# A recurrence on eight columns: one PSUM bank per gate, inputs grouped in one step, expert work woven into the routing

## The reference, cut to what matters

```
for t in range(256):                       # h: 8 batches x 128
    r = sigmoid(x[t] @ W_ir + b_ir + h @ W_hr)
    z = sigmoid(x[t] @ W_iz + b_iz + h @ W_hz)
    n = tanh(x[t] @ W_in + b_in + r * (h @ W_hn + b_hn))
    h = (1 - z) * n + z * h
# every token (2048 of them): softmax over h @ router_w.T, top-1 expert;
# an expert takes at most 320 tokens, those of highest probability,
# and the rest go to expert 0
# y = relu(h @ W1[e] + b1[e]) @ W2[e] + b2[e],  W1 128x512, W2 512x128
```

## Time and profile before

| | us |
|---|---|
| median of 3 runs (lowest to highest) | 1527.37 (1525.01 to 1528.93) |
| the profiled execution, its own time | 1528.47 |
| its span, first to last instruction | 1526.7 |
| PE busy in the span | 1403.5 (92%) |
| DVE, ACT, POOL busy | 715.6, 673.6, 146.7 |
| mean granted TensorE clock | 0.944 of full speed |
| DMA, mean over the span | 18 GB/s |

### The profile page before, as it was taken

One profiled execution on the slowest core, in us unless ns is written; L12 is line 12 of the kernel. 1 busy time (PEld: TensorE's weight loads), 2 busy tenths in 40 slices (PEclk: granted clock), 3 DMA queues, 4 the chain that ended last, 5 costly groups with the idle time before them and its releaser, 6 DMA issues. The chain is left out here.

```text
span 1526.7 us, 29728 instructions
## 1 busy us (share of the span) xinstructions
PE 1403.5 (92%) x10828; PEld 1104.6 (72%) x10829; DVE 715.6 (47%) x2422; ACT 673.6 (44%) x2429; POOL 146.7 (10%) x236
## 2 busy tenths in 40 slices
PE   7999988999989999999999997699999999838994
PEld 4333333777769999999999983488888888735663
DVE  3476765545543454444544526532333333672223
ACT  3322213556534666666666641243434443623442
POOL 4000003000000000000000000110000000325652
PEclk9899989999999999999999986697999999968997
DMA  5000000000021000000000000100000000001113
GB/s 164 1 1 0 1 0 1 1 1 1 1 70 43 2 1 2 2 2 2 2 2 2 2 1 1 35 22 22 23 23 22 23 9 2 12 18 38 42 42 98
DMA packets 27834, 27.93 MB, mean 18 GB/s; under 512 B 2381, under 2 KB 22346, under 8 KB 27562
## 3 DMA queue, kind: packets, MB, share of 16 engines
q1 hardware_dynamic: 21082, 16.71, 3.7%
q0 software_dynamic: 2496, 5.12, 1.2%
q10 hardware_dynamic: 4112, 4.19, 0.9%
HBM read 21.36 MB, written 4.65 MB: 17 GB/s over the span
## 5 line engine op out<-in xcount | busy, mean ns | idle before, releaser
L1698 PE MATMUL spare<-identb 128*128 128x128 bf16 x2996 | 215.1, 223 | 0.0
L1698 PEld LDWEIGHTS spare<-identb 128*128 128x128 bf16 x2996 | 198.6, 106 | 4.7
L1186 ACT ACTIVATE ghid<-gh_ps,cols 128x128 f32<-128x128 f32 x512 | 160.3, 364 | 63.7 <-PE gh_ps L1094 63.7
L1094 PE MATMUL gh_ps<-hist,w 128*128 128x128 f32 x1024 | 160.5, 278 | 2.9 <-ACT ghid L1186 2.9
L1104 PE MATMUL gy_ps<-w2e,ghid 128*128 128x128 f32 x1024 | 156.2, 275 | 0.5 <-ACT ghid L1186 0.3
L1094 PEld LDWEIGHTS gh_ps<-hist,w 128*128 128x128 f32 x1024 | 136.5, 189 | 5.3 <-ACT ghid L1186 5.2
L1104 PEld LDWEIGHTS gy_ps<-w2e,ghid 128*128 128x128 f32 x1024 | 135.5, 191 | 0.9 <-ACT ghid L1186 0.5
L1147 PE MATMUL pre_z<-hist,gru_w 128*128 128x128 f32 x512 | 121.5, 318 | 0.0
L1758 DVE TENSOR_TENSOR_SCAN targ<-gates,pairs 128x16 f32<-128x16 f32 x256 | 49.1, 192 | 149.0 <-ACT gates L1708 149.0
L1655 PEld LDWEIGHTS s_pre<-s,wT 128*128 128x128 f32 x512 | 80.1, 197 | 42.1 <-ACT s L1711 40.1
L1655 PE MATMUL s_pre<-s,wT 128*128 128x8 f32 x512 | 100.7, 269 | 4.4 <-ACT s L1711 2.7
(11 more groups left out here) (422 smaller groups left out, 2458.8 us busy)
## 6 DMA issues: line engine op xcount, KB each, us to landing
w<-in_L_ffn_W SPq DMA_DIRECT2D x1, 2048.0 KB, 9.6
raw<-in_L_ffn_wg SPq DMA_DIRECT2D x8, 256.0 KB, 3.1
raw<-in_L_ffn_wu SPq DMA_DIRECT2D x8, 256.0 KB, 3.1
raw<-in_L_ffn_wd SPq DMA_DIRECT2D x8, 256.0 KB, 2.6
wqkv<-in_L_attn_Wqkv SPq DMA_DIRECT2D x1, 1536.0 KB, 6.3
mrow<-mt SPq DMA_DIRECT2D x8, 128.0 KB, 1.8
y_top<-yrow SPq DMA_DIRECT2D x4, 256.0 KB, 5.4
y_next<-yrow ACTq DMA_DIRECT2D x4, 256.0 KB, 6.2
```

The lines of the kernel that those rows point to most:

```text
L1094: mm = nc.tensor.matmul(h_ps[:, f % 2, :], w1[:, e, P * f:P * f + P], tokens(grp), start=True, stop=True)
L1186: nc.scalar.activation(hid[v % 2][:, f, :], h_ps[:, f % 2, :], ACT.Relu, bias=n.cols[:, at:at + 1]).then_inc(h_done, 1)
L1698: nc.tensor.matmul(spare[:, 0:P], n.identb[:, :], n.identb[:, :], start=True, stop=True)
```

## The change

`gru_scan` and `route_top1` become one function, `recurrence`.

- A gate has one bank instead of two, and `pre_z` is a product of 8 columns as the other two are. `hist` is no longer set to zero but for its first step.
- The seven input products of the next group are issued together behind step 15 of a group, each gate's behind a wait for the engine that last read that gate's bank. There is no expert step in that step of the recurrence. So 225 of the 260 expert steps lie within the recurrence (there were 240).
- `gh_ps` and `gy_ps` have two banks each within the recurrence and one afterwards. The transposes, choices and logits share another bank in four slots.
- The logits: POOL copies each finished group of 16 steps into `hB` in another layout (16 copies of 128 by 128), and the router's products take their weights from there; the 8 blocks of the first half are woven into the recurrence, one at a time, and 8 are left behind the last step.
- The other 35 expert steps are woven into the routing: 2, 4 and 2 into its first block, one for each of the 24 pieces into the second, and 3 behind them. `rows` has two buffers instead of three.
- `picks` and `parts` have 128 columns instead of 24, with zeros in the rest, and so have the transposes and the products made of them.

```diff
+    def expert_step(s):
+        return (s // G - 1) * (G - 1) + s % G if s >= G and s % G != FREE else None
...
+                @block.gpsimd
+                def _(pool):
...
+                    for g in range(GROUPS):
+                        pool.wait_ge(state, G * (g + 1) + 1)
+                        pool.tensor_copy(hB[:, :, G * g:G * g + G], tokens(g).rearrange("p (t b) -> p b t", b=B)).then_inc(turned_b, 1)
...
+                    def inputs(g, s):
...
+                        if s >= 0:
+                            pe.wait_ge(r_done, s + 1)
+                        nc.tensor.matmul(pre_r[:, 0:P], n.gru_w[:, 0, :], x, start=True, stop=False, skip_group_check=True)
+                        nc.tensor.matmul(pre_r[:, 0:P], n.bias_parts[:, 1, :], n.ones_b[:, :], start=False, stop=False, skip_group_check=True)
...
                         pe.wait_ge(state, s + 1)
-                        for out, i, rhs, ready in ((gate_slot(pre_r, s), 3, now, r_pre), (first(n_slot(s)), 5, now, n_pre),
-                                                   (z_out, 4, h, z_pre)):
-                            nc.tensor.matmul(out, n.gru_w[:, i, :], rhs, start=False, stop=True,
+                        for out, i, ready in ((gate_slot(pre_r, s), 3, r_pre), (first(n_slot(s)), 5, n_pre), (gate_slot(pre_z, s), 4, z_pre)):
+                            nc.tensor.matmul(out, n.gru_w[:, i, :], now, start=False, stop=True,
                                              skip_group_check=True).then_inc(ready, 1)
...
+                        if s % G == FREE:
+                            if s // G + 1 < GROUPS:
+                                inputs(s // G + 1, s)
+                        elif s < G:
+                            for _ in range(FILL):
+                                nc.tensor.matmul(y_bank[0][:, 0:P], n.identb[:, :], n.identb[:, :], start=True, stop=True)
+                        else:
+                            w = expert_step(s)
...
+                            expert_products(pe, w)
+                            grp, k = divmod(w, G)
+                            if GROUPS // SEG + 2 <= grp < GROUPS // SEG + 2 + B // 2 and k in (8, 12):
...
+                                block_logits(SEG * (2 * (grp - GROUPS // SEG - 2) + (k == 12)))
...
                 @block.tensor
                 def _(pe):
-                    for src, dst, ready in ((picks, tq, 6), (parts, tp, 14)):
+                    w = w0
+                    for src, dst, ready, ahead in ((picks, tq, 6, EARLY), (parts, tp, 14, MIDDLE)):
+                        for _ in range(ahead):
+                            expert_products(pe, w)
+                            w += 1
                         pe.wait_ge(step, ready)
...
+                    step_no = w1st
                     for r in range(NP):
                         i, c0, w, _ = pieces[r]
+                        if step_no < STEPS:
+                            expert_products(pe, step_no)
+                            step_no += 1
                         pe.wait_ge(counted, r + 1)
+                        if r + 2 < NP:
+                            fill(r + 2)
...
-                        if r + 3 < NP:
-                            fill(r + 3)
```

More of the change, by code:

```diff
@@ L979, in _, with recurrence @@
                     add(b)
-def gru_scan(nc, n, a, hist, w1, w2, diffT, logits):
+def recurrence(nc, n, a, hist, w1, w2, diffT):
     G = P // B
@@ L1003, in sem, with bank @@
             return local.enter_context(nc.semaphore(name))
[L1005 to L1018, removed]
+        def bank(name, stack=local):
+            return stack.enter_context(nc.psum_tensor(name, [P, 512], F32))
+        h_bank, y_bank, turn = [bank("gh_ps0")], [bank("gy_ps0")], bank("g_turn")
+        slot = [turn[:, P * i:P * i + P] for i in range(4)]
         hid = [sb(f"ghid{i}", [P, NF, P]) for i in range(2)]
@@ L1047, in tokens @@
             return second(hist[:, 16 * (G * g + 1):16 * (G * (g + 1) + 1)])
[L1049 to L1140, removed]
@@ new lines, in expert_relu @@
+        def expert_relu(act, w):
+            if w >= HALVES:
+                return
+            v, half = divmod(w, 2)
+            e = v % E
+            act.wait_ge(h_in, w + 1)
+            if v >= 2:
+                act.wait_ge(y_in, v - 1)
+            for f in range(2):
+                at = b10 + NF * e + 2 * half + f
+                nc.scalar.activation(hid[v % 2][:, 2 * half + f, :], h_bank[w % len(h_bank)][:, P * f:P * f + P], ACT.Relu,
+                                     bias=n.cols[:, at:at + 1]).then_inc(h_done, 1)
@@ L1148, in _ @@
                                              skip_group_check=True).then_inc(ready, 1)
[L1149 to L1156, removed]
@@ L1170, in _ @@
+                    pe.wait_ge(state, T + 1)
+                    for b in range(B):
+                        mm = block_logits(SEG * b + 1)
+                    mm.then_inc(all_logits, 1)
+                @block.scalar
+                def _(act):
+                    act.preload_act_table(ACT.Sigmoid)
+                    act.wait_ge(const, 4)
+                    for s in range(T):
                         act.wait_ge(r_pre, s + 1)
@@ new lines, in _ @@
+                        w = expert_step(s)
+                        if w is not None:
+                            expert_relu(act, w)
+                @block.vector
+                def _(dve):
+                    V = nc.vector
+                    for i in range(2):
+                        V.memset(reset[i][:, :], 0.0)
+                        V.memset(fresh[i][:, :], 0.0)
+                        last = V.memset(mix[i][:, :], 0.0)
+                    V.memset(choice[:, :], 0.0)
+                    last.then_inc(const, 1)
+                    V.tensor_scalar(iota_m8[:, :], n.iota8[:, :], -float(E), None, ALU.add).then_inc(const, 1)
+                    V.tensor_scalar(zero_hot[:, :], n.iota8[:, :], 0.0, None, ALU.is_equal).then_inc(const, 1)
+                    V.memset(at_step(0), 0.0).then_inc(const, 1)
+                    dve.wait_ge(const, 4)
+                    V.tensor_copy(second(at_step(0)), n.condT).then_inc(state, 1)
+                    dve.wait_ge(state, 1)
+                    for s in range(T):
@@ L1274, in _ @@
-                    v = (s - G) // 2 - 1
-                    if k % 2 == 0 and 0 <= v < JOBS:
-                        add(v)
-                    if k == 0 and grp < GROUPS:
-                        choose(grp, 0)
-                    if k == 1 and grp < GROUPS:
-                        for i in range(1, 4):
-                            choose(grp, i)
-                    if s == T + 1:
-                        dve.wait_ge(all_logits, 1)
-                        V.tensor_copy(logits[:, :, :].rearrange("p i e -> p (i e)"), pre_r[0][:, 0:NBLK * E])
@@ L1402, in route_top1 @@
         NP = len(pieces)
+        w1st = w0 + EARLY + MIDDLE + LATE
         with ExitStack() as middle:
-            rows = [middle.enter_context(nc.psum_tensor(f"rows{i}", [P, PIECE], F32)) for i in range(3)]
+            rows = [middle.enter_context(nc.psum_tensor(f"rows{i}", [P, PIECE], F32)) for i in range(2)]
             sums = middle.enter_context(nc.psum_tensor("r_sums", [P, 512], F32))
```

369 lines of the change are left out of this document (220 added, 149 removed).

## The result

| | before | after |
|---|---|---|
| median of four runs on one chip, us | 1528.15 | 1864.16 |
| lowest to highest | 1525.01 to 1529.22 | 1861.83 to 1869.25 |
| span of the profiled execution | 1526.7 | 1867.4 |
| mean granted TensorE clock | 0.944 | 0.755 |

The ratio is 1.221, 95% interval 1.219 to 1.224. The forecast was 1507.4, in 1492 to 1527.

What follows compares the result with a forecast made beforehand. Plain steps were taken as bound by the state's chain, 0.06 us above TensorE's work. Terms -17.8 - 30.8 + 10.1 + 16.8 + 1.7 = -20.0 us on the 1527.4 median gave 1507.4, range 1492 to 1527.

Steps and rivals of the forecast that it cites:

- `pre_z` on 8 columns: Recurrence: dropping 120 columns shortens the product's end by about 0.10 us, gaining 0.065 us for each plain step.
- The clock falls inside the recurrence: Rival, recurrence: shorter `pre_z` lowers the clock; steps over 2 us, time far over 1600 us; chance 2%.
- the slower rival of the routing: Rival, routing behind the recurrence: woven work runs at 1.2 GHz, +33 us, so 1540; chance 0.11.
- recurrence: All groups of steps together: -17.8 us, from shorter plain steps and input products gathered into one step.
- behind the last step: Stage after the recurrence: 34.1 us replaced by 3.3 for the last copy and remaining logits, -30.8 us.
- first routing block: Routing's first block: eight added expert steps take it from 8.9 to 19 us, +10.1, between +6 and +13.
- loop of the second: Routing's second block, 24 pieces: TensorE becomes the limit at 1.6 us a piece; 27.3 to 44.1 us, +16.8.
- Plain step: Recurrence step without input products: 1.64 us set by the state's chain becomes 1.575, set by TensorE's 14 passes.
- Input step: Step 15 of a group, all inputs and no expert work: 1.59 to 1.77 us, 1.77 taken.
- The rival that the step stays at 1.64: Recurrence: the 128 columns weren't in the chain, so plain steps gain nothing; +14.6 us, 1522; chance 0.14.
- POOL's copies: Recurrence, 16 a group: about 0.35 us each, counted as nothing; up to 5.6 us worse if all contend with VectorE.
- "better weave" rival: Routing's second-block loop: coupling costs nothing and VectorE's 31.8 + 1 sets it; 11 us less, 1496; chance 0.12.

Runs made afterwards that it cites:

- experiments 2: Kernel before with only its update gate product `pre_z` narrowed to 8 columns: 1894.71 us, ratio 1.246.
- 7: Changed kernel with two 128-column bf16 fillers in each of the first 128 expert steps: 1884.36 us.
- experiment 1: Changed kernel with 72 small filler products at the head of TensorE's list of the recurrence: 1493.21 us, ratio 0.982.
- experiment 5: Changed kernel with 72 fillers at the recurrence's head and the update gate on 128 columns again: 1504.96 us, ratio 0.989.
- experiment 12: Changed kernel with 72 head fillers, routing's turned operands back on 24 rows: four executions, 1492.03, 1495.97, 1509.32 and 1514.92 us.
- experiment 11: Changed kernel with 72 head fillers plus fillers in TensorE's later idle stretches up to the next layer: 1491.83 us.
- experiment 6: Changed kernel with one burst of 80 fillers at the end of step 127: 1682.02 us.
- experiment 3: Changed kernel with its update gate on 128 columns again and the history zeroed beforehand: 1535.30 us, ratio 1.008.
- 9: Changed kernel with the first hidden product issued twice (float32) in the first 128 expert steps: 1575.43 us.
- 10: Changed kernel with twelve 128-column bf16 fillers in each of the first 32 expert steps: 1539.70 us, one execution; a second, 5889 us, left out.
- 4: Kernel before without the 16 fillers in each of its first 16 steps: 1535.49 us, ratio 1.009.

## Why the prediction was wrong

**The step that failed** is the first of the change, "*`pre_z` on 8 columns*", where I priced the 120 columns as the end of a product and nothing else, and its rival "*The clock falls inside the recurrence*", to which I gave 2% because "the expert products, which make up most of a step, are untouched". They are eight of 14 passes, and TensorE is always busy, and still such a step does not raise the clock (the changed kernel, experiments 2 and 7). In place of a plain step of 1.575 us the runs show one of 2.99, at 0.50 for 802 us, and a recurrence that is 352 us longer where the sum had -17.8. The price in the rival was right in kind: it had steps over 2 us, and a step at half clock is 14 passes at 0.2135, 2.99. Its mechanism was put wrongly: the clock doesn't fall in the recurrence, it is low on entry and is not raised. I argued from the stretch 762 to 890.7, where the clock had been full for 300 us, and never asked from what it had come up. The trace of before had the warning at 452.5: it enters low, and something in its first steps has to raise it. One row warned too. Behind the last step TensorE was busy for 10.2 us at 0.50 before the clock came back. I put that down to expert steps, to argue *against* the slower rival of the routing; but the first half of it, to 897.7, is the router's products, which are 8 columns wide.

The Trainium skill (TensorE: Matmul & The Clock Gate, "Why this matters for your kernels") says to keep TensorE continuously busy for full clock, and to avoid idle gaps. The second half agrees: behind the gap of 4.9 us ahead of the recurrence the clock is at 0.50 (from 452.5 in the kernel before). The first half doesn't hold here: TensorE is shown busy for all of 282.00 us (480 to 762) at 0.50.

**The other terms** can be read from experiment 1, which is the change at full clock, against the earlier trace rows:

| us | forecast | experiment 1 |
|---|---|---|
| recurrence | -17.8 | 415.2 - 435.1 = -19.9 |
| behind the last step | -30.8 | 3.4 - 34.1 = -30.7 |
| first routing block | +10.1 | 16.6 - 8.9 = +7.7 |
| loop of the second | +16.8 | 36.6 - 27.3 = +9.3 |
| end, to the next layer's first product | +1.7 | 11.9 - 9.0 = +2.9 |
| sum | -20.0 | -30.7 |

The two profiled executions are 33.9 us apart (1528.47 and 1494.56). The other 3.2 us lie outside the change: the first state comes 0.7 us later in experiment 1, and the layers behind the routing take some 4 us less; why was not followed.

- *Plain step* 1.575: right (1.57), and bound by TensorE. *Input step* 1.77: right (1.78). The rival that the step stays at 1.64 is refuted by experiment 5 against 1.
- *POOL's copies* are 0.40 each (0.35 taken). None of them overlaps an instruction of VectorE in experiment 1 or in the changed kernel, and the recurrence came out better than the sum: there is no loss of 5.6 us, but no run shows the two together either.
- *Behind the last step*: right; the 16 weight loads of the logits took 2.12 us, not 1.8.
- *First block*: within its bounds, at full clock but for its first 5.5 us.
- *Loop*: mis-sized. I had 1.6 a piece by TensorE, and 5.7 on top for coupling, start, once-a-group products and half clock. It measured 36.6 / 24 = 1.53 a piece, all included, 7.5 us less: TensorE's own work is 35.38, not 38.4, and all the rest is 1.2. That is the way of the "better weave" rival, but not its mechanism. It had VectorE as the limit, and VectorE is busy 31.34 of the 36.6 (31.8 forecast), while TensorE is the limit still.
- *Slower: the woven routing at 1.2 GHz*: not in the changed kernel (clock 0.97 in its loop), but real. The profiled execution of experiment 12 shows it, for 20 us, where I had priced 33.

Had the recurrence entered at full clock, the time would have been 1493, just inside the range and 14 us below the likeliest, by a loop that was mis-sized.

## What to carry to other kernels

TensorE being always busy does not say that it will reach full clock: this stream of products held the high clock when it had it, and could not raise the low one. So when an edit makes products narrower, look at the clock where its loop *begins*, not in its middle, and at what TensorE did before. If it comes out of a wait, a few us of small products in that wait are cheap insurance: here 72 of them turned 1864 us into 1493, and that is the version to keep (experiment 11's 1491.8 can't be told from it).

## What the hardware showed that I had not expected

- Two clocks for one and the same instruction stream: 2.99 and 1.57 us a step, each kept for over 200 us in one execution (experiment 6, 0.50 and 1.00).
- A TensorE that shows as busy all of the time did not raise the clock in 802 us. In experiment 3 two passes of a step had 128 columns instead of 8, in 9 two more float32 passes of 128 columns were added, in 10 twelve bf16 products, and the clock rose; with two bf16 products (7) it didn't. Which property counts was not settled; that the fillers' weights and data are an identity matrix wasn't separated from their type.
- An 8-column float32 pass takes as long as a 128-column one in TensorE's queue, 0.11 at full and 0.2135 at half clock: at half clock a plain step is 2.99 with `pre_z` on 8 columns and in experiments 3 and 4 with it on 128. The zero columns cost 10 to 13 us of 1505 there, and did a job that no line of the code mentions.
